# A transformer layer's prologue on one core, rebuilt: sets of loads, a smaller shear, keys rotated on VectorE

## The reference

```python
q, k, v = heads(xn @ Wq + bq), heads(xn @ Wk + bk), heads(xn @ Wv + bv)    # 16 heads of 16
q = q * cos + rotate_half(q) * sin;  k = k * cos + rotate_half(k) * sin    # rotary positions
att = softmax((q @ k.T + rel_bias_table[bucket(i - j)]) / 4, causal)
attention = (att @ v) @ Wp + bp

logits = l2norm(xn) @ l2norm(col_emb).T + sigmoid(gelu(xn @ gate_w1 + gate_b1) @ gate_w2 + gate_b2)
weights = softmax(logits) where logits is its row's maximum, else 0        # one of 16 columns per token
cols = gelu(einsum('bsd,cdn->bscn', xn, W_cols) + b_cols) * weights
ffn = layer_norm(cols.reshape(B, T, 1024) @ proj_w + proj_b + xn) * ln_g + ln_b
```

## Time and profile before

| | us |
|---|---|
| median of 3 runs | 2038.77 (2036.24 to 2040.76) |
| the profiled execution | 2044.04 |
| its span | 2042.2 |
| PE busy in the span | 1845.2 (90%) |
| DVE busy | 1603.7 (79%) |
| ACT busy | 1109.9 (54%) |
| POOL busy | 648.7 (32%) |

### The profile page before, as it was taken

How to read it: one execution, slowest core, us unless ns; L and a number is a source line. 1 busy time by engine, 2 the same in 40 slices (tenths; PEclk the granted TensorE clock), 3 DMA queues, 4 the chain that set the end, 5 groups by cost and what they waited for, 6 DMA issues and landing times.

```text
span 2042.2 us, 41462 instructions
## 1 busy us (share of the span) xinstructions
PE 1845.2 (90%) x10854; PEld 1027.4 (50%) x10854; DVE 1603.7 (79%) x5475; ACT 1109.9 (54%) x2146; POOL 648.7 (32%) x848
## 2 busy tenths in 40 slices
PE   4779999999999999999999999999999999999886
PEld 2435555555555545555545555555455555445432
DVE  1457888888888888878888888878888888878783
ACT  2324555565555556555556555556655555655544
POOL 4643233333332333332332333233333223301110
PEclk9879999999999999999999999999999999999998
DMA  7642322332233332333233323333223322322201
GB/s 218 207 128 63 89 73 76 115 95 81 78 95 96 91 89 82 92 93 102 59 94 108 92 80 90 87 85 104 84 74 93 103 83 77 89 78 69 57 16 47
DMA packets 217028, 185.61 MB, mean 91 GB/s; under 512 B 61931, under 2 KB 196475, under 8 KB 216780
## 3 DMA queue, kind: packets, MB, share of 16 engines
q1 hardware_dynamic: 216780, 182.75, 30.9%
HBM read 115.23 MB, written 72.94 MB: 92 GB/s over the span
## 4 chain that ended last, share of the span: by engine, by line
PE 63%; DVE 19%; issue 9%; ACT 4%; DMA 2%; SPq 2%; POOL 1%; DVEq 1%; ACTq 0%; POOLq 0%
PE o_bank L1080 11%; PE rows L1096 11%; PE scores L1063 9%; PE scores L1155 8%; PE bank L1166 8%; PE bank L1109 7%; DVE scores L1227 3%; PE bank L1184 3%; DVE maxima L1253 3%; ACT probs L948 3%; DVE rows L1248 3%; PE scores L1157 2%; PE scores L1117 1%; DMA x<-in_x_dram 1%; DVE maxima L1248 1%
## 5 line engine op out<-in xcount | busy, mean ns | idle before, releaser
L948 ACT ACTIVATE probs<-scores 128x512 f32<-128x512 f32 (+1 forms) x1280 | 669.8, 556 | 465.9 <-DVE scores L1227 222.6
L1253 DVE TENSOR_REDUCE maxima<-rows 128x1 f32<-128x384 f32 (+4 forms) x896 | 479.4, 551 | 176.2 <-PE rows L1096 175.4
L1063 PE MATMUL scores<-stack_q,stack_k 99*128 99x512 bf16 (+3 forms) x1536 | 438.2, 335 | 75.5 <-ACT probs L948 69.6
L1096 PE MATMUL rows<-stack_k,stack_q 96*128 96x256 bf16 (+3 forms) x2048 | 464.8, 293 | 24.1 <-issue 10.8
L1248 DVE CUSTOM_DVE_ANT_0 rows<-rows,near_rows 128x256 f32<-128x256 f32 (+1 forms) x1024 | 393.9, 431 | 53.9 <-PE rows L1096 48.3
L1096 PEld LDWEIGHTS rows<-stack_k,stack_q 96*128 96x128 bf16 x2048 | 177.6, 98 | 365.2 <-issue 150.3
L1227 DVE TENSOR_TENSOR scores<-scores,near_cols 128x256 f32<-128x256 f32 x768 | 324.3, 433 | 22.2 <-PE scores L1063 22.0
L1080 PE MATMUL o_bank<-probs,v_aug 128*32 128x512 f32 (+3 forms) x3072 | 321.6, 506 | 2.8 <-ACT probs L948 2.8
L1166 PE MATMUL bank<-w_proj,act_t 128*128 128x256 f32 x1024 | 259.2, 387 | 24.6 <-DVE y L1283 24.6
L1155 PE MATMUL scores<-again,w_cols 128*128 128x256 f32 x1024 | 273.5, 389 | 0.0
L1063 PEld LDWEIGHTS scores<-stack_q,stack_k 99*128 99x128 bf16 x1536 | 144.0, 99 | 236.0 <-ACT probs L948 167.4
(11 more groups left out here) (112 smaller groups left out, 2019.7 us busy)
## 6 DMA issues: line engine op xcount, KB each, us to landing
parts_d<-part SPq DMA_DIRECT2D x96, 256.0 KB, 2.3
stack_q<-parts_d SPq DMA_DIRECT2D x384, 64.0 KB, 2.7
stack_k<-parts_d SPq DMA_DIRECT2D x384, 64.0 KB, 2.6
kept_d<-kept SPq DMA_DIRECT2D x31, 512.0 KB, 3.0
again<-kept_d SPq DMA_DIRECT2D x31, 512.0 KB, 3.8
x<-in_x_dram SPq DMA_DIRECT2D x32, 256.0 KB, 3.5
v_d<-v SPq DMA_DIRECT2D x32, 256.0 KB, 2.4
rest<-in_x_dram SPq DMA_DIRECT2D x32, 256.0 KB, 4.5
```

The costliest lines, as they stand in the source:

```text
L948: act.activation(probs[:, (g * NS + s) % PROBS, h, 0:width], ring[(rings + ring_n[1]) % RING][:, 0:width], ACT.Exp, scale=float(D) ** -0.5 ...
L1063: ins = pe.matmul(ring[(rings + ring_n[1]) % RING][:, c0:c0 + w], stack_k[g % 2][:, h, kb * P:(kb + 1) * P], stack_q[g % 2][:, h, q0:q0 + ...
L1096: ins = pe.matmul(tile[:, at:at + k1 - k0], stack_q[ag % 2][0:STACK, h, qb * P:(qb + 1) * P], stack_k[ag % 2][0:STACK, h, k0:k1], start=Tr ...
L1253: ins = dve.tensor_reduce(maxima[:, part, m:m + n], tile[:, at:at + n * w].rearrange("p (n w) -> p n w", w=w), AX.X, ALU.max)
```

## The change

Six things change, all in the prologue and the set-up.

- The 21 loads become three sets with a semaphore each: five for the set-up (`setup_in`), issued by ACT's queue; five that `qk` needs (`qk_weights_in`), behind x of chunk 1 on SP; eleven others (`weights_in`), awaited where they are first used. ACT no longer waits for the write of the offsets, DVE fills `v_aug` in POOL's place, and b_cols is loaded ahead of W_cols.
- The shear keeps 32 copies in place of 128 (`SHEARED`), and eight loads of 32 partitions read them; they come with chunk 2's `x_turn`.
- In chunks -5 to -2 DVE rotates the keys (`turn`), POOL the queries only. In chunk -1 and the loop POOL rotates both.
- The first group's second half of the stacks is loaded as two pieces, chunk by chunk (`load_part`), 12 transfers each.
- Its rows come in three sets (`FIRST_ROWS`): 12 early, 12 middle (kinds 3, 5, 6) and 16 last.
- The neurons of the first chunk move behind chunk -2, among the early rows; chunk -1 lies among the middle rows, the columns and what follows among the last. Four neuron pieces of the second chunk lie between `shift` and `shift_turn`.

```diff
+    between(-5, {"next gate": [("skip", -2, None)]})
+    between(-4, {"next v 1": [("load_q", -2, None), ("load_k", -2, None)]})
+    between(-3, {"next v 1": [("load_part", -2, 2)]})
...
+    spread(each(-2, "qk_turn 0, left 0, middle 0, qk_turn 1, left 1, middle 1") + [("load_part", -2, 3)], [])
+    spread(neurons[0] + each(-1, "center"), rows[0])
+    spread(each(-2, "choose, load_v") + each(-1, "x_turn, qk_begun 0, qk 0") + each(-2, "tie")
+           + each(-1, "qk_begun 1, qk 1") + each(-2, "choice") + each(-1, "v 0, v 1, load_q, load_k, rest_in")
+           + each(-2, "mask_turn") + each(-1, "hidden, gate"), rows[1])
+    spread(columns + each(-1, "choose, qk_turn 0, left 0, middle 0, y2_stats, ffn_in, qk_turn 1, left 1, middle 1, tie, "
+                          "load, skip, widen, load_v") + [("stats", 0, None)] + neurons[1][:4], rows[2])
+    spread([("shift", -1, None)] + neurons[1][4:] + each(-1, "finish, shift_turn") + [("center", 0, None)], [])
...
-            for r in range(2):
+            for r in (1, 0):
                 sp.dma_start(sheared_d[r], bass.AP(offsets_d.tensor, r * (H * N_OFF + P),
-                                                   [[N_OFF, H], [0, P], [1, SHEAR]])).then_inc(sheared, 16)
+                                                   [[N_OFF, H], [0, SHEARED], [1, SHEAR]])).then_inc(sheared, 16)
...
+                for r, near in ((1, near_rows), (0, near_cols)):
+                    for p in range(0, P, SHEARED):
+                        sp.dma_start(near[p:p + SHEARED, :, :],
...
+                    elif stage == "load_part":
+
+                        landed = quarter_in if arg == 2 else stack_in[0]
+                        for i in range(3):
+                            sp.wait_ge(parts_out[i], (arg + 1) * 16)
...
+            act.dma_start(qk[0:BUCKETS + 1, :, :], a["offset_picks"]).then_inc(setup_in, 16)
+            act.dma_start(y2[0:BUCKETS, 0, 0:H], a["rel_bias_table"]).then_inc(setup_in, 16)
+            act.dma_start(act_t[0:E, 0, :], a["col_emb"]).then_inc(setup_in, 16)
+            act.dma_start(ident[:, :], a["ident"]).then_inc(setup_in, 16)
+            act.dma_start(act_t[0:E, 1:5, :].rearrange("p m n -> p (m n)"), a["pick"]).then_inc(setup_in, 16)
...
+                    elif stage == "turn":
+
+                        i, use = bank_use(bank_n, needs)
+                        at = (n * CT + arg) * 3
+                        dve.wait_ge(bank_drained[i], use + 2)
+
+                        wait(dve, hi_ready, n * CT + (arg + 1 - CT))
+                        for op, args in swaps(arg, c, slice(C, 2 * C)):
+                            ins = dve.tensor_tensor(*args, op)
+                        ins.then_inc(turn_step, 1)
+                        dve.wait_ge(turn_step, at + 1)
+                        dve.tensor_tensor(*by_cos(arg, c, slice(C, 2 * C)), ALU.mult).then_inc(turn_step, 1)
+                        dve.wait_ge(turn_step, at + 2)
+                        dve.tensor_tensor(*added(arg, slice(C, 2 * C)), ALU.add).then_inc(turn_step, 1)
```

More of the change, by code:

```diff
@@ L154 @@
 NEURONS = [("neurons", (k, m)) for k in range(EM // N_PIECES) for m in range(N_PIECES)]
-FIRST = ["stats", "center", "x_turn", "qk_begun 0", "qk 0", "qk_begun 1", "qk 1", "v 0", "v 1", "hidden", "gate"]
+FIRST = ["stats", "center", "x_turn", "qk_begun 0", "qk 0", "turn 0", "qk_begun 1", "qk 1", "turn 1", "v 0", "v 1",
+         "hidden", "gate"]
 BETWEEN = ["next center", "choose", "next x_turn", "qk_turn 0", "left 0", "middle 0", "later stats", "tie",
-           "next qk_begun 0", "next qk 0", "qk_turn 1", "left 1", "choice", "middle 1", "next qk_begun 1", "next qk 1",
-           "mask_turn", "next v 0", "next v 1", "next hidden", "next gate"]
-FINAL = [stage for stage in BETWEEN if stage.split()[0] not in ("next", "later")]
+           "next qk_begun 0", "next qk 0", "qk_turn 1", "left 1", "next turn 0", "choice", "middle 1",
+           "next qk_begun 1", "next qk 1", "next turn 1", "mask_turn", "next v 0", "next v 1", "next hidden",
+           "next gate"]
 CLOSING = [("load", None), ("load_v", None), ("neurons", (0, 0)), ("neurons", (0, 1)), ("pv", NS - 1), ("o_out", 1),
@@ L221, in add @@
             needs = self.used["qk_turn", arg]
+        if stage == "turn":
+            needs = self.used["qk", arg]
         if stage == "gate":
@@ L295, in between, with spread, each @@
                 o.add(stage, at, arg)
+    def spread(stages, rows):
+        done = 0
+        for at, (stage, g, arg) in enumerate(stages):
+            o.add(stage, g, arg)
+            upto = len(rows) * (at + 1) // len(stages)
+            for row in rows[done:upto]:
+                o.add("row", -1, row)
+            done = upto
+    def each(g, text):
+        return [(stage, g, int(arg[0]) if arg else None) for stage, *arg in map(str.split, text.split(", "))]
     for stage in FIRST:
@@ L300, in prologue @@
             o.add("stats", -4)
[L301 to L323, removed]
@@ L324, in prologue @@
-    o.add("shift_turn", -1)
+    between(-5, {"next gate": [("skip", -2, None)]})
+    between(-4, {"next v 1": [("load_q", -2, None), ("load_k", -2, None)]})
+    between(-3, {"next v 1": [("load_part", -2, 2)]})
+    early, last = GH * len(EARLY), GH * len(LAST)
+    rows = FIRST_ROWS[:early], FIRST_ROWS[early:-last], FIRST_ROWS[-last:]
+    neurons = [[(stage, g, arg) for stage, arg in NEURONS] for g in (-2, -1)]
+    columns = [("columns", -1, k) for k in range(C_PIECES)]
+    spread(each(-2, "qk_turn 0, left 0, middle 0, qk_turn 1, left 1, middle 1") + [("load_part", -2, 3)], [])
```

209 lines of the change are left out of this document (131 added, 78 removed).

## The result

The changed kernel takes 2024.0 us (median; 2015.2 to 2030.3) against 2038.2 (2034.2 to 2043.9): a ratio of 0.9932, with a 95% interval from 0.9918 to 0.9945, 14 us faster. The forecast was 2015.5 with a range of 2005 to 2026. The time lies in the range, 8.5 us above the forecast and nearest to the second rival (2022). The profiled execution took 2023.29 us, its span 2021.5.

The account below looks back on a forecast made before the run. The prologue, until the first score at 175.32 us, was taken as bound by four waits in a row, not PE. Gains of 18.7 up to chunk 4's centring and 4.5 after make 23.2, giving 2015.5 us, range 2005 to 2026.

Parts of the forecast that it names:

- the second rival: Prologue: x or near loads stay late, or DVE and GpSimd block fully; gain 17, 2022 us; chance 0.22.
- The start: Set-up loads on ACT's queue: set-up from 6.9 us instead of 17.95, bounds 5 and 9.5; first chunk 11 us sooner.
- supply and demand: x of chunk 3: its landing (supply, 33.1) and DVE's readiness for it (demand, 33.6) meet; gain there 22.0 us.
- The turns: DVE rotating keys in the first chunks: 1.45 us per tile plus 0.6 of blocking; period 16.2 us, bounds 14 and 19.
- 1.45 us per tile: DVE's own time to rotate one tile's keys, two swaps and two operations, with overlap and waits.
- I add 0.6 us: Per tile, DVE and GpSimd waiting for each other during the rotation; bounds 0 and 2.15.
- The centring gave back: A chunk's centring on DVE meets less GpSimd work and gives back 1.4 us per period; pairs near 0.8.
- The near loads: Moved to chunk 2's x_turn, about 32 us, with parts and values queued behind: cost 1 us, bounds 0 and 6.
- x or the near loads stay late: Chunk 3 at 39 us, or periods of 19 if DVE and GpSimd block fully; gain 17, 2022 us; chance 0.22.
- the likeliest case: The forecast itself: gain 23.2 us, 2015.5 us, by itself 2011 to 2020; chance 0.52.
- The rest: Chunk 4's centring to first score, stage by stage: 93.7 us becomes 89.2, gain 4.5.
- the slower one: PE's lower clock over the prologue's last stages: a loss of 37 us, 2052 us; chance 0.03.

Follow-up runs that it names:

- near_split: Changed kernel with near loads apart: near_rows behind the second chunk's parts, near_cols behind the last stack piece; 2015.33 us, ratio 0.9886 to the kernel before.
- shear128: Changed kernel with 128 shear copies again in place of 32, and two near loads in place of eight; 2026.77 us, one execution.
- near_back: Changed kernel with all eight near loads moved back behind the second chunk's parts; 2028.46 us, ratio 0.9941 to the kernel before.
- before_shear32: Kernel before with 32 shear copies alone, eight near loads in their old place; 2036.95 us, ratio 0.9987 to the kernel before.

## Why the prediction was right, and where it was off

The mechanism is as forecast in the main: what the prologue saves goes forward. The first score comes 15.6 us earlier (means of two profiles each), and the time is 14.2 less. Behind it little changed: the span less the first score is 1862 and 1864 us in the two profiles of after and 1867 in both of before, and 1858 to 1868 over all kernels. The gain was forecast as 23.2 us, and the 2024.0 lies in the range because that was wide and because one error made up for part of the others; it lies outside the 2011 to 2020 that the forecast had by itself. In the prologue the forecast was too large by 7 us, the sum of four terms:

- **The start** was to be at 6.9 and came at 9.42, at the upper bound given (9.5). 2.5 us off, and all of it is in the 2.4 us by which chunk 3's statistics missed 33.6. That supply and demand meet there was right: DVE waited 0.40 us. The shear writes landed in 6.9 us (forecast under 8).
- **The turns.** "1.45 us per tile" was 1.65 alone, "I add 0.6 us" was 1.1. Chunk 3's centring came 14.3 behind its statistics (forecast 12.1) in one profile and 14.8 in the other: 2.2 us off. The centring gave back what was said or more (pairs of 0.73). The period without the near loads' wait is 16.1 to 18.0 (near_split, 17.2 on average) where 16.2 was forecast. The traces agree with the Trainium skill (SBUF — State Buffer, Who interferes with whom) that a DVE instruction with two SBUF inputs contends with GpSimd's reads; for the period it was worth less than the 18 to 19 worked out from it.
- **The near loads** are the step that failed: "5.2 MB in all at the 299 GB/s ... end at 49.4: I take 1 us, bounds 0 and 6". Chunk 4's centring came 7.4 us later behind chunk 3's than forecast, 1 us for them included, so past the upper bound. Both factors were off. From 32.0 to 61.3, when the first part landed, the core moved 231 GB/s, so 6.8 MB and not 5.2: other traffic, such as the 512 KB stores of `kept`, shares the engines. At 299 GB/s that would have ended near 54.6, an estimate from these rows; the other 6.7 us are the rate. The 299 was measured on two loads of 128 partitions from 128 copies, and the change itself replaced them by eight of 32 from 32 copies, which move at 196. The issue wasn't priced either (12.2 us for the eight, 8.23 for the three writes behind them). But the DMA engines were full all that time, so it isn't shown to add anything to the transfers, and shear128 has 9.24 us of issue at the same place and no wait. This step put the time on the second rival, "x or the near loads stay late", rather than on the likeliest case.
- **The rest** gave more: 93.7 to 84.3, 9.4 us where 4.5 was forecast. By stages: 18.2 for 16.9, 15.1 for 15.3, 16.0 for 17.5, 26.6 for 28.5, 8.4 for 10, and no cost for the clock shows in these sums (1 allowed). The fifth chunk and everything behind it is where the sum was too careful. The stacks stalled nobody, as forecast.

2.4 + 2.2 + 7.4 - 4.9 is 7.1 of the 8.5 us. Against the rivals: the slower one didn't come, since PE's clock was 0.66 from 133 to 148, where DVE bounds the rows, but 1.00 from 93.2 to 108.3 and from 150.9 on, where the neurons are.

What stays open: why PE's clock is lower with all keys on GpSimd, so that the stretch from centring 4 to the first score takes 90.3 us where it takes 81.8 with the turns, and with it whether the turns are worth anything. The time says no (0.9886 both), and three placements of them don't differ by more than their intervals. Also open is why the near loads are slower in their new form.

## What to carry to other kernels

Price a moved DMA by the rate of its new shape, not of its old one, together with everything else that moves in the same stretch; and ask which small stores stand behind it on its queue. A block of loads that fills the DMA engines is paid for by the stores behind it whose buffers the next stage waits for. Moving the block moves the wait to the next store; splitting it, with each part behind a store that matters, removed it. An edit that saves bytes in one place (a quarter of the shear) can cost rate in another (the loads that read it). And a gain at the head of a chain of chunks reaches the end only if the transfers keep up: 13 us at chunk 3 were 5 to 7 at the first score in one kernel here.

## What the runs showed of the hardware

- The near loads, 4 MB in pieces of 1 KB, moved at 346 GB/s as two DMAs of 128 partitions from 128 copies (shear128, DMA share 1.08) and at 350 in the kernel before (1.09), and at 195 to 198 as eight of 32 partitions from 32 copies (after twice, near_back, before_shear32; 1.13 to 1.14).
- The issue time of a DMA on SyncE depends on what is in flight. Three 256 KB stores of parts took 1.71 and 2.57 us to issue later in the changed kernel's prologue, and 8.23 us behind the near loads (9.24 in shear128, behind only two). A store of v took 0.34 us in the changed kernel, and 3.21 behind them in near_back.
- DVE's product of two SBUF operands of 128x256 took 0.43 us with GpSimd idle and 0.93 beside it, the sum 0.62 and 1.46, a pair of swaps of 128x128 0.60 and 1.11. A centring pair, with one SBUF tensor as input, took 0.73 us or 2.99, the latter beside GpSimd's rotation over 512 columns. The Trainium skill (SBUF — State Buffer, Who interferes with whom) names both cases, the second as a tensor_scalar in a mode of two ports. The traces agree that the two engines hinder each other; that DVE's product and sum end just behind GpSimd's operation fits a blocking for nearly its whole length. No row shows which mode the centring runs in.
- The changed kernel's time spreads over 15 us (2015.2 to 2030.3), the kernel before's over 10.
